# Layer 3's second feed-forward product: plain f32 on unsplit tiles instead of two fp32r products on split tiles

## The reference, cut to what matters

```python
xn = _layernorm(x, axis=-1)
x = x + _L3_attn_ref(xn, ...) + _L3_ffn_ref(xn, L3_ffn_w_gate_up, L3_ffn_w_proj)

def _L3_ffn_ref(x, w_gate_up, w_proj):
    wq_gu = ternary_quant(w_gate_up)
    gu = jnp.einsum('bsd,hd->bsh', x, wq_gu)
    gate, up = jnp.split(gu, 2, axis=-1)
    h = jax.nn.silu(gate) * up
    hn = rms_norm(h)
    wq_p = ternary_quant(w_proj)
    return jnp.einsum('bsh,dh->bsd', hn, wq_p)
```

## Time and profile before

| | |
|---|---|
| times of three runs | 736.20, 737.72, 739.47 us |
| their median | 737.72 us |
| the profiled execution's own time | 739.46 us |
| its span, first to last instruction | 737.4 us |
| mean granted clock of TensorE | 0.962 of full speed |
| busy share of the span: PE, DVE, ACT, POOL | 89%, 71%, 47%, 43% |
| layer 3's units, first to last instruction | 640.5 to 734.9 us |

### The profile page before, as it was taken

The page is one execution under the profiler, slowest core; times in us unless marked ns, Lnnn a source line. Parts: engine busy times, 40 slices in busy tenths (PEclk is TensorE's granted clock), DMA queues, the critical chain, the costliest instruction groups (busy, mean ns, idle before and its releaser), DMA issues. The chain is left out here.

```text
span 737.4 us, 13276 instructions
## 1 busy us (share of the span) xinstructions
PE 656.1 (89%) x4740; PEld 492.9 (67%) x4740; DVE 520.9 (71%) x1064; ACT 347.6 (47%) x749; POOL 319.6 (43%) x255
## 2 busy tenths in 40 slices
PE   4978999999789999999999999889986799867788
PEld 1434555578368887878797887779865547545666
DVE  4176667673589979797979987366266774569794
ACT  1465212120446475656555574644364352297732
POOL 1000698600267657474747576696148331300100
PEclk9998999999899999999999999999999799989889
DMA  8601000000500101000000101114202100100001
GB/s 263 290 1 59 1 1 1 1 1 1 188 34 24 36 21 36 5 22 30 21 36 21 36 23 34 44 36 154 58 9 72 43 1 1 36 0 1 1 0 58
DMA packets 14645, 31.34 MB, mean 43 GB/s; under 512 B 1837, under 2 KB 8587, under 8 KB 14029
## 3 DMA queue, kind: packets, MB, share of 16 engines
q1 hardware_dynamic: 12813, 26.46, 10.6%
q0 software_dynamic: 1536, 3.15, 1.5%
q10 hardware_dynamic: 256, 1.18, 0.6%
HBM read 26.59 MB, written 5.24 MB: 43 GB/s over the span
## 5 line engine op out<-in xcount | busy, mean ns | idle before, releaser
L573 PE MATMUL bank<-zone 128*128 128x256 f32 (+1 forms) x408 | 142.0, 348 | 21.8 <-DVE zone L1642 5.5
L574 PE MATMUL bank<-zone 128*128 128x256 f32 (+1 forms) x408 | 133.6, 327 | 0.0
L575 PE MATMUL bank<-zone 128*128 128x256 f32 (+1 forms) x408 | 133.3, 327 | 0.0
L2042 POOL TENSOR_TENSOR arena<-arena 128x512 f32<-128x512 f32 x64 | 82.2, 1285 | 89.5 <-ACT arena L1233 89.5
L573 PEld LDWEIGHTS bank<-zone 128*128 128x128 f32 x408 | 79.0, 194 | 43.1 <-issue 17.2
L2047 POOL TENSOR_TENSOR arena<-arena 128x512 f32<-128x512 f32 x64 | 83.2, 1301 | 31.9 <-DVE arena L1626 22.3
L575 PEld LDWEIGHTS bank<-zone 128*128 128x128 f32 x408 | 79.2, 194 | 6.4
L574 PEld LDWEIGHTS bank<-zone 128*128 128x128 f32 x408 | 79.2, 194 | 3.6
L554 PE MATMUL bank<-xT,arena 128*128 128x512 f32 x160 | 79.5, 637 | 2.0 <-ACT xT L1122 1.5
L1252 ACT ACTIVATE arena<-arena 128x256 f32<-128x256 f32 (+1 forms) x128 | 62.0, 487 | 31.6 <-DVE arena L1635 31.0
L1651 DVE SCALAR_TENSOR_TENSOR x<-bank,arena,x 128x256 f32<-128x256 f32 x128 | 53.0, 470 | 20.3 <-PE bank L575 19.4
(11 more groups left out here) (287 smaller groups left out, 1332.3 us busy)
## 6 DMA issues: line engine op xcount, KB each, us to landing
arena<-in_qk SPq DMA_DIRECT2D x16, 256.0 KB, 2.8
arena<-in_tern SPq DMA_DIRECT2D x1, 3072.0 KB, 22.3
arena<-in_wv SPq DMA_DIRECT2D x8, 256.0 KB, 2.8
arena<-in_wo SPq DMA_DIRECT2D x16, 128.0 KB, 2.1
arena<-in_wr SPq DMA_DIRECT2D x1, 1792.0 KB, 11.2
lB<-in_lB SPq DMA_DIRECT2D x1, 1288.5 KB, 24.8
x<-in_x SPq DMA_DIRECT2D x2, 512.0 KB, 8.0
xg_rows<-arena SPq DMA_DIRECT2D x1, 1024.0 KB
```

Source lines behind the costliest of these rows:

```text
L573: pe.matmul(dst, lhi, rhi, start=(n == 0), stop=False)
L574: pe.matmul(dst, lhi, rlo, start=False, stop=False)
L575: last = pe.matmul(dst, llo, rhi, start=False, stop=(n == len(terms) - 1 and not open_end))
L2042: pool.tensor_tensor(qraw[:, j, :], qraw[:, j, :], cosT[:, at], ALU.mult).then_inc(cos_done, 1)
```

## The change

The four-deep `hid3` and the two six-deep rings of fp32r parts are replaced by one six-deep ring of plain f32 tiles, which lies in the same memory under a second name (`plain`), since no tile of it is written as fp32r. The roundings (L1399, 16 on ACT) and the rests (L1867, 16 on DVE) are gone, with their two semaphores. `collect` has 4 matmuls of 128x256 in f32 where it had 8 in fp32r, and waits for `hidden(n)` itself. `hidden(n)` waits, from unit 6 on, for the square and the product of unit n - 6, whose tile it overwrites. `hidden_of`, with its two parts of x, stays as it is. No instruction changes places otherwise.

```diff
+        with nc.sbuf_tensor("plain", [P, ZONE], F32) as plain:
+            pass
         zone = sb("zone", ZONE)
...
-        hid3 = m.grid(4, BW)
...
-        hid3p = [z.grid(RING3, BW) for _ in range(2)]
+        hid3 = Carve(plain, z.at).grid(RING3, BW)
...
             def collect(n):
 
                 b, q = divmod(n, NI)
-                pe.wait_ge(hid3_split, n + 1)
+                pe.wait_ge(*g_gu3[n][1].ready)
...
                     for tt in range(2):
-                        for m, part in enumerate(parts(hid3p)):
-                            last = pe.matmul(g.ps[:, tt * D:(tt + 1) * D], part[:, n % RING3, tok(2 * p + tt)], pr_T[:, q, :].bitcast(F32R),
-                                             start=(q == 0 and tt == 0 and m == 0), stop=(q == NI - 1 and tt == 1 and m == 1), skip_group_check=True)
+                        last = pe.matmul(g.ps[:, tt * D:(tt + 1) * D], hid3[:, n % RING3, tok(2 * p + tt)], pr_T[:, q, :],
+                                         start=(q == 0 and tt == 0), stop=(q == NI - 1 and tt == 1), skip_group_check=True)
...
-                act.activation(hsq3[n % RING3], hid3[:, n % 4, :], ACT.Square).then_inc(hsq_ready, 1)
-                if n >= RING3:
-                    act.wait_ge(*given_back(hid3_used, n - RING3, [g[1] for g in g_down3]))
-                act.activation(hid3p[0][:, n % RING3, :].bitcast(F32R), hid3[:, n % 4, :], ACT.Copy).then_inc(hid3_hi, 1)
+                act.activation(hsq3[n % RING3], hid3[:, n % RING3, :], ACT.Square).then_inc(hsq_ready, 1)
...
-            def rest_of_hidden(n):
-                dve.wait_ge(hid3_hi, n + 1)
-                dve.tensor_tensor(hid3p[1][:, n % RING3, :].bitcast(F32R), hid3[:, n % 4, :], hid3p[0][:, n % RING3, :], ALU.subtract).then_inc(hid3_split, 1)
-
             def hidden(n):
...
-                if n >= 4:
-                    dve.wait_ge(hid3_split, n - 3)
-                dve.tensor_tensor(hid3[:, n % 4, :], g.ps, silu3[:, n % 2, :], ALU.mult).then_inc(g.ready_sem, 1)
-                if 1 <= n <= NI - 2 or n > NI:
-                    rest_of_hidden(n - 1)
+                if n >= RING3:
+                    dve.wait_ge(hsq_ready, n - RING3 + 1)
+                    dve.wait_ge(*given_back(hid3_used, n - RING3, [g[1] for g in g_down3]))
+                dve.tensor_tensor(hid3[:, n % RING3, :], g.ps, silu3[:, n % 2, :], ALU.mult).then_inc(g.ready_sem, 1)
```

More of the change, by code:

```diff
@@ L221, in build @@
         qk_full, v_full, wv_hi, wv_split = sem("qk_full"), sem("v_full"), sem("wv_hi"), sem("wv_split")
-        win3_hi, win3_split, hid3_hi, hid3_split, hid3_used = (
-            sem("win3_hi"), sem("win3_split"), sem("hid3_hi"), sem("hid3_split"), sem("hid3_used"))
+        win3_hi, win3_split, hid3_used = sem("win3_hi"), sem("win3_split"), sem("hid3_used")
         hre3_ready = sem("hre3_ready")
@@ L1949, in _ @@
             hidden(7)
-            rest_of_hidden(6)
-            rest_of_hidden(7)
             re, im, xr, xi, tmp = c3[11], c3[8], c3[0], c3[1], c3[9]
@@ L1986, in _ @@
                 hidden(n)
-            rest_of_hidden(UNITS - 1)
             for p in range(NT // 2 - 1):
```

## The result

| | before | with the change |
|---|---|---|
| median of five runs | 737.89 us | 740.76 us |
| lowest to highest | 736.20 to 739.47 us | 740.17 to 742.46 us |
| profiled execution, and its span | 739.46, 737.4 us | 740.67, 738.6 us |

The ratio is 1.0044, with a 95% interval of 1.0026 to 1.0062: slower by 2.9 us and clear of noise. The ratio lies just inside half a per cent; its interval reaches past it. The forecast was 741.5 us (+3.8), its range 738.0 to 744.0.

What follows compares the result with a forecast made beforehand. VectorE was taken as the limit in the first stretch, TensorE alone from `hidden(9)` to the end. Gain, dearer products and slack, -2.55 + 6.56 - 0.23 = +3.8 us, on 737.7 gave 741.5 us, range 738.0 to 744.0.

Steps and rivals of the forecast that it cites:

- The price: Second product in plain f32: 0.82 us more per `collect`, 13 us in 16, by the nearest row, `project_h`.
- rival (d): A plain record costs 0.2175 us, 0.78 more per `collect`: +3.3 us, 741.0; chance 0.52 together with the forecast.
- Step 1: From `hidden(2)` to `keep_sum(0)`: TensorE runs without waits, VectorE ahead of it; `keep_sum(0)` at 683.65, 2.55 us gained.
- Step 2: From `keep_sum(0)` to `hidden(9)`: the chain moves 2.55 us sooner as a whole; cost 0, 0.8 us of cover left.
- Step 3: From `hidden(9)` to the end: TensorE has no idle time, so dearer products count fully, 6.56 us through `collect(15)`.
- Rests 8 to 15 go from VectorE and bring nothing: Behind `hidden(9)`: 4.8 us of rests leave VectorE without gain, because it waits for TensorE.
- The second stretch costs 1.5 us: The 1.2 GHz clock from 705.20 to 708.50 costs 1.5 us of bound work; one such stretch left in.
- Rival (c): Behind the wait for `hidden(9)`, the slow clock lasts twice as long on bound work: +5.3 us, 743.0; chance 0.20.
- Case (b): No slow-clock stretch falls on bound work: +2.3 us, 740.0; chance 0.20.
- Rival (a): VectorE keeps the pace, plain product near its low price, TensorE's chain does not grow: 3.8 us faster, 733.9; chance 0.08.

Runs made afterwards that it cites:

- e3: Against the kernel before: units 0 to 7 plain, without roundings and rests; units 8 to 15 still split. 735.62 us, ratio 0.9971.
- e7: Against the kernel before: units 0 to 7 plain, units 8 to 15 split, plus unread filler matmuls in TensorE's waits. Ratio 0.9941.
- e1: Against the changed kernel: tile written as fp32r, each second-product matmul done twice in fp32r with it; roundings and rests stay out. 733.37 us, ratio 0.9945 to before.
- e12: Against the changed kernel: the 16 roundings and rests still made into unread scratch tiles, plus filler matmuls in TensorE's waits. 741.40 us, ratio 1.0054 to before.
- e6: Against the changed kernel: 22 unread filler matmuls added in TensorE's waits. Ratio to before 1.0007.
- e8: Against the kernel before: unread filler matmuls (12, 4 and 16) added in TensorE's waits, nothing else. Ratio 1.0000.
- e9: Against e1: the same two fp32r products without roundings or rests, plus filler matmuls in TensorE's waits. 730.38 us, ratio 0.9917 to before.
- e5: Against e1: one fp32r product per tile instead of two, rests left out of the sum. 734.16 us, ratio 0.9897 to before.
- e10: Against e5: the same single fp32r product per tile, plus filler matmuls in TensorE's waits. 728.19 us, ratio 0.9867 to before.
- e4: Against the kernel before: units 0 to 7 still split, units 8 to 15 plain. 745.91 us, ratio 1.0120.
- e11: Against e4: the same split units 0 to 7 and plain units 8 to 15, plus filler matmuls in TensorE's waits. 742.88 us, ratio 1.0079 to before.
- e2: Against the changed kernel: the 16 roundings and 16 rests still made into scratch tiles that nobody reads. 746.46 us, ratio 1.0120 to before.

## Why the prediction was right, and where it was off

- **The price.** "0.82 us more per `collect`", taken from `project_h`: it is 0.77, the value of the long run in layer 0 that I had named and passed over. The row misled by one record: of `project_h`'s 16 from 725.65 on, the first, which stands behind `sum_features`, takes 0.32 us to the next one's start, and the other 15 take 0.216, as do the 24 of `collect` above. The low side, rival (d), is the one that came; the two records per matmul were right, and so was the estimate of 0.427 us per matmul beside the sum (0.432 measured).
- **Step 1.** TensorE without waits from unit 4 on, VectorE ahead of it, `keep_sum(0)` held by TensorE's sum: all as forecast. The size was 2.92 against 2.55, five products at the lower price (5 x 0.05 = 0.25) and somewhat shorter units. `hidden(6)` came 3.84 us sooner behind `hidden(0)` (21.72 for 25.56), for the 3.74 of rests and wait. e3 and e7 show that this gain comes with block 0 alone; e1, where `keep_sum(0)` comes 4.0 us sooner, shows that TensorE's dearer products held it in the change. No run takes out the roundings alone or the rests alone: that the gain is VectorE's is read from the traces.
- **Step 2.** Cost 0, and 0.83 us of cover left (forecast 0.8). `hidden(9)` came 2.90 sooner.
- **Step 3.** TensorE without idle time to the end: right. Behind `hidden(9)` +5.67 was measured and 6.56 - 0.23 = 6.33 forecast. 0.4 of the difference is the price (8 x 0.05). That `add_ffn(1)` would wait for `collect(15)` was wrong: GpSimd still released it, as its first two operations need the first bank only, which is full halfway through `collect(15)`. The last `add_pair` waits for `project_h(3)` instead (0.56 us).
- **"Rests 8 to 15 go from VectorE and bring nothing"** held with the plain product: the stretch takes 34.26 us with them (e12) and without (e6). **"The second stretch costs 1.5 us"** held for the change (1.3, e6) and not for the kernel before, where taking it away brings nothing (e8), since VectorE with its rests needs the same 29.9 us. The step that was wrong is the one under both, that TensorE was the only limit behind `hidden(9)`. It cost the forecast nothing only because the two limits of the kernel before happened to lie within 0.01 us: that is luck. With the clock full in both kernels the same working gives -2.9 + 5.9 = +3.0, and e6 against e8 measures +1.4, as 1.5 us come from the rests that go. Rival (c), a longer slow stretch, did not come: the clock was 1.00 again from 703.50 on. Case (b), the change without a slow stretch, is +1.4 in e6 against before, for +2.3: the forecast's excess (3.8 for 2.8 by the marks), with 1.3 for 1.5 of slow clock.
- **Rival (a)**, VectorE keeps the pace and the kernel gets faster, fails on the price. With 8 fp32r records per tile (e1) `hidden(9)` does come 4.0 us sooner, as worked out; that the whole then came out 4.1 us faster, for 3.8, is in part luck, since behind `hidden(9)` the trace of e1 lost 1.2 us to the clock and that of e9, with fillers, won 1.5. The rule that would have TensorE's headroom judged by load time (the Trainium skill, "Perfetto Trace Analysis", Identifying the Most-Contended Engine, which names the share of peak FLOP/s beside it, not worked out here) misled. Loads were busy for 25.46 of 31.50 us while TensorE was the bound with no idle time, since the plain product has as many loads as the split one and takes nearly twice as long.
- **The total.** +2.9 us, by ratio and by the marks, for +3.8 forecast: right in direction and in where the gain and the loss lie, a quarter too large, and on the other side of the 0.5% that I had put just under the forecast. That TensorE alone could stand for the second half was luck, as said above.

## What to carry to other kernels

Trading two cheap products for one dear one pays where the engine that makes the split is the bound and not where TensorE is: here the same edit won 2.9 us in one block and lost 4.4 in the next, so it belongs in block 0 only. An engine without idle time is a limit, but not proof that it is the only one: when two engines are both full over a stretch, taking work from one brings nothing until the other gets less too, and a run that makes one of them cheaper shows how far apart they are. And where TensorE has waited before bound work, look at its granted clock first; differences of 1 to 3 us between traces here came from there and not from the edit.

## What the runs showed of the hardware

A plain f32 matmul of 128x256 shows as two records of 0.216 us each at 2.4 GHz, against one of 0.120 us in fp32r: one plain matmul costs 3.6 of fp32r, and 1.8 times the two of them that the split needs.

Independent matmuls in TensorE's waits (22 to 34 of 128x512 in fp32r) went with a granted clock of 1.00 from `sum_squares(0)` to the last `add_pair` in the traces of six of the seven kernels that have them (one execution each). They gave back 1.1 to 2.7 us where the stretch behind them got shorter (e5 to e10: 27.15 to 26.01; e3 to e7: 31.14 to 29.90; change to e6: 35.58 to 34.26; e4 to e11: 35.87 to 34.27; e1 to e9: 31.08 to 28.37; e2 to e12: 37.00 to 34.26) and nothing where another engine was as long (before to e8).

Not every fall of the clock stood behind a long wait. In e11_back_fill it fell after 3.60 us in which TensorE was busy for 1.75. In e12_rests_fill it fell once behind a stretch without idle time (`collect(5)` to `collect(7)`, the 16 one-column records of `sum_squares(0)` and the first fillers):

```profile
690.00:697.50 7.50, 7.48 (x43) 6.41 (x42) 4.31 (x4) 7.41 (x8) 0.00 (x0) 1.00 0.01 2
697.96:701.30 3.34, 3.34 (x9) 2.56 (x9) 3.34 (x6) 1.53 (x3) 1.42 (x1) 0.50 0.02 5
```

TensorE was busy for 7.48 of 7.50 us, and the clock was 0.50 soon after. It was back before `hidden(9)` at 705.89, so the marks of e12 are not touched by it. e6_after_fill has the same operations in the same order there, and its clock stayed 1.00. I have no explanation from these runs.
